# Normalise-and-project stages of a transformer kernel: the two halves of the tokens taken in another order

## The reference

```python
x = x + L0_xattn(_layernorm(x, axis=-1), ctx_768, ...)
x = x + L0_attn(_layernorm(x, axis=-1), ...)
x = x + L0_ffn(_layernorm(x, axis=-1), ...)
...
```

## Time and profile before

| | before |
|---|---|
| median of 3 runs | 2348.39 us (2341.73 to 2354.28) |
| the profiled execution | 2342.55 us |
| its span, first to last instruction | 2340.7 us |
| PE busy | 75% of the span |
| DVE busy | 46% |
| ACT busy | 32% |
| POOL busy | 22% |
| TensorE's granted clock, mean | 0.84 of full speed |

### The profile page before, as it was taken

One profiled execution on the slowest core, in us unless ns is written; L12 is line 12 of the kernel. 1 busy time (PEld: TensorE's weight loads), 2 busy tenths in 40 slices (PEclk: granted clock), 3 DMA queues, 4 the chain that ended last, 5 costly groups with the idle time before them and its releaser, 6 DMA issues. The chain is left out here.

```text
span 2340.7 us, 55956 instructions
## 1 busy us (share of the span) xinstructions
PE 1745.5 (75%) x22746; PEld 1508.6 (64%) x22746; DVE 1082.4 (46%) x2292; ACT 760.0 (32%) x1679; POOL 521.9 (22%) x683
## 2 busy tenths in 40 slices
PE   5997537689957886847884799673898676867684
PEld 4886436579946775637774688553787565756673
DVE  5565572411147775162114466537466445334313
ACT  3554332134424453302332455322142222323121
POOL 3442321022223331003442222100021222010142
PEclk9998755689979998758997899986889898776697
DMA  3110000179921110017995111001011211000385
GB/s 135 53 48 15 1 1 4 43 283 342 351 85 52 44 38 5 3 57 244 309 301 194 29 47 45 21 0 39 26 45 55 55 54 45 3 2 4 126 282 180
DMA packets 86641, 214.54 MB, mean 92 GB/s; under 512 B 20113, under 2 KB 38897, under 8 KB 78897
## 3 DMA queue, kind: packets, MB, share of 16 engines
q1 hardware_dynamic: 78288, 189.43, 24.8%
q0 software_dynamic: 8160, 22.29, 2.9%
HBM read 196.17 MB, written 15.34 MB: 90 GB/s over the span
## 5 line engine op out<-in xcount | busy, mean ns | idle before, releaser
L2184 ACT ACTIVATE g<-ps,b 128x128 f32<-128x128 f32 x340 | 125.0, 368 | 286.6 <-PE ps L2146 265.5
L2146 PEld LDWEIGHTS ps<-xt,w 128*128 128x128 f32 x1728 | 212.2, 197 | 8.3 <-issue 4.1
L2146 PE MATMUL ps<-xt,w 128*128 128x128 f32 x1728 | 213.3, 280 | 2.2 <-DVE xt L2325 2.1
L2156 PE MATMUL ps<-w,g 128*128 128x256 f32 x864 | 202.9, 382 | 0.0
L2156 PEld LDWEIGHTS ps<-w,g 128*128 128x128 f32 x864 | 158.4, 191 | 18.4
L449 PE MATMUL ps<-x,w 128*128 128x512 f32 x432 | 132.8, 476 | 38.9 <-DVE x L538 38.9
L2202 POOL DMA_INDIRECT x<-rows,token x85 | 83.3, 980 | 307.3 <-DVEq L2301 273.6
L2207 POOL DMA_INDIRECT results<-y,dest x85 | 83.7, 985 | 280.9 <-DVE y L2338 223.0
L2325 DVE COPY xt<-ps 128x256 f32<-128x256 f32 x85 | 36.1, 425 | 235.8 <-PE ps L2136 235.8
L449 PEld LDWEIGHTS ps<-x,w 128*128 128x128 f32 x432 | 100.9, 238 | 68.5 <-DVE x L538 44.6
L433 PE MATMUL ps<-consts_sb,z_sb 128*128 128x128 f32 x176 | 35.3, 370 | 115.0 <-DVE z_sb L524 115.0
(11 more groups left out here) (411 smaller groups left out, 4042.3 us busy)
## 6 DMA issues: line engine op xcount, KB each, us to landing
w<-in_L_ffn_w SPq DMA_DIRECT2D x124, 512.0 KB, 4.9
w<-in_L_ffn_w SPq DMA_DIRECT2D x46, 1024.0 KB, 7.4
c<-in_ctx SPq DMA_DIRECT2D x128, 258.0 KB, 2.7
b<-in_w_L_ffn SPq DMA_DIRECT2D x62, 128.0 KB, 6.5
back<-results SPq DMA_DIRECT2D x16, 256.0 KB, 5.0
raw<-in_L_ffn_w SPq DMA_DIRECT2D x16, 256.0 KB, 2.8
rows<-z_sb SPq DMA_DIRECT2D x3, 1024.0 KB, 4.4
back<-results SPq DMA_DIRECT2D x8, 384.0 KB, 6.5
```

The lines of the kernel that those rows point to most:

```text
L2146: mm = nc.tensor.matmul(hidden_bank(par, h), b.w1[:, par, c, h * P:(h + 1) * P], b.xt[:, par, c, :], start=c == 0, stop=c == DC - 1)
L2156: mm = nc.tensor.matmul(k.ps[:, YB + par, 0:D], b.g[:, par, h, :], b.w2[:, par, h, :], start=h == 0, stop=h == HC - 1)
L2184: nc.scalar.activation(b.g[:, par, h, :], hidden_bank(par, h), func, bias=b.b1[:, par, h:h + 1]).then_inc(s.g_ready, 1)
```

## The change

Only `prepare` is edited. In each of its 14 calls:

- ACT first waits for the `eps` constant, runs a one-column square root (`b.warm`) and then rounds the first weight matrix only. It takes the deviation of the first half, copies the first half's turned activations, takes the deviation of the second half, rounds the other weight matrices, evicts the first product if it owns it, copies the second half's turned activations and evicts the rest.
- DVE takes the statistics of the first half, normalises it, takes the statistics of the second half, computes the first half's low parts, normalises the second half, evicts the first product if it owns it, computes the second half's low parts and evicts the rest. Without products the order is: statistics, norm, statistics, norm, and the two copies at the end.
- PE turns the first half, makes the first unit of the first half, turns the second half, makes the other units of the first half and those of the second.
- POOL and SP are unchanged.

```diff
+            turn(0)
+            if units:
+                product(0, 0)
+            turn(1)
+            for n in range(1, len(units)):
+                product(0, n)
+            for n in range(len(units)):
+                product(1, n)
...
+            act.wait_ge(s.eps_set, 1)
+            nc.scalar.activation(b.warm[:], b.eps[:], ACT.Sqrt)
+            if w_at:
+                act.wait_ge(*w_at)
+            if ws:
+                round_weights(0)
+            deviation(0)
+            take_turned(0)
+            deviation(1)
+            for n in range(1, len(ws)):
+                round_weights(n)
+            if units:
+                take_product(0, 0)
+            take_turned(1)
+            for n in range(1, len(units)):
+                take_product(0, n)
+            for n in range(len(units)):
+                take_product(1, n)
...
+            nc.vector.memset(b.eps[:], LN_EPS).then_inc(s.eps_set, 1)
+            statistics(0)
+            norm(0)
+            statistics(1)
             if w_at:
                 dve.wait_ge(*w_at)
...
+            if jobs:
+                split(0)
+            norm(1)
+            if jobs:
+                take_product(0, 0)
+                split(1)
+                for n in range(1, len(units)):
+                    take_product(0, n)
+                for n in range(len(units)):
+                    take_product(1, n)
+            else:
+                take_turned(0)
+                take_turned(1)
```

More of the change, by code:

```diff
@@ L396, in prepare @@
     with stage(k, names) as (block, s), ExitStack() as ctx:
-        b = ctx.enter_context(buffers(k, stats=[P, NT, 6], mv=[P, NT, 2], std=[P, NT], rstd=[P, NT], eps=[P, 1]))
+        b = ctx.enter_context(buffers(k, stats=[P, NT, 6], mv=[P, NT, 2], std=[P, NT], rstd=[P, NT], eps=[P, 1], warm=[P, 1]))
         if jobs:
@@ L428, in _, with turn @@
         def _(pe):
-            for half in range(2):
+            def turn(half):
                 for t in range(HT):
@@ L435, in _, with product @@
                 mm.then_inc(s.turned, 1)
[L436 to L444, removed]
+            def product(half, n):
+                kind, wi, _, _, _, at = units[n]
+                if n == 0:
+                    pe.wait_ge(s.x_lo, DC * (half + 1))
+                if half == 0:
+                    pe.wait_ge(s.w_split, wi + 1)
+                turn_ = half * len(units) + n
+                if turn_ >= BANKS:
+                    pe.wait_ge(*taken((turn_ - BANKS) % len(units), (turn_ - BANKS) // len(units)))
+                bank = k.ps[:, 4 + turn_ % BANKS, :]
+                if kind == "channel":
+                    col = starts[wi] + at * P
@@ L445, in _ @@
                     for i, (p1, p2) in enumerate(TERMS):
                         for c in range(DC):
[L447 to L450, removed]
-                                                      start=i == 0 and c == 0, stop=i == 2 and c == DC - 1)
@@ L452, in _ @@
[L452 to L459, removed]
@@ L460, in _ @@
-                    mm.then_inc(s.product_done, 1)
+                            mm = nc.tensor.matmul(bank, r.w[:, p1, c, col:col + P],
+                                                  r.x[:, p2, c, half * 512:(half + 1) * 512],
+                                                  start=i == 0 and c == 0, stop=i == 2 and c == DC - 1)
+                else:
+                    for t in range(2):
+                        tok = (half * HT + 2 * at + t) * P
+                        for i, (p1, p2) in enumerate(TERMS):
+                            for c in range(DC):
+                                mm = nc.tensor.matmul(bank[:, t * D:(t + 1) * D], r.x[:, p1, c, tok:tok + P],
+                                                      r.w[:, p2, c, starts[wi]:starts[wi] + D],
+                                                      start=i == 0 and c == 0, stop=i == 2 and c == DC - 1)
@@ L462, in _ @@
+                mm.then_inc(s.product_done, 1)
+            turn(0)
[6 more added lines that the diff above has]
+                product(1, n)
         @block.scalar
         def _(act):
[L464 to L467, removed]
@@ L468, in _, with round_weights, deviation @@
-            act.wait_ge(s.eps_set, 1)
-            for half in range(2):
+            def round_weights(n):
+                nc.scalar.copy(r.w[:, HI, :, starts[n]:starts[n + 1]], ws[n]).then_inc(s.w_hi, 1)
+            def deviation(half):
                 tiles = slice(half * HT, (half + 1) * HT)
@@ L472, in _, with take_turned @@
                 nc.scalar.activation(b.std[:, tiles], b.mv[:, tiles, 1], ACT.Sqrt, bias=b.eps[:, 0:1]).then_inc(s.std_done, 1)
-            for half in range(2):
+            def take_turned(half):
                 tokens = slice(half * 512, (half + 1) * 512)
@@ L487, in _, with take_product @@
                             nc.scalar.activation(out, inp, ACT.Identity, bias=shift[:, c:c + 1], scale=gain[:, c:c + 1])
[L488 to L498, removed]
+            def take_product(half, n):
+                kind, _, _, bias, scale, m = units[n]
+                if owner[n] == "dve":
+                    return
+                act.wait_ge(s.product_done, half * len(units) + n + 1)
+                out, inp = view(n, half)
+                if kind == "token":
+                    nc.scalar.copy(out, inp).then_inc(s.taken_act, 1)
+                elif bias is None:
+                    nc.scalar.mul(out, inp, scale).then_inc(s.taken_act, 1)
+                else:
+                    nc.scalar.activation(out, inp, ACT.Identity, bias=bias[:, m:m + 1]).then_inc(s.taken_act, 1)
+            act.wait_ge(s.eps_set, 1)
[16 more added lines that the diff above has]
+                take_product(1, n)
         @block.gpsimd
@@ L510, in _, with statistics @@
         def _(dve):
-            nc.vector.memset(b.eps[:], LN_EPS).then_inc(s.eps_set, 1)
-            for half in range(2):
+            def statistics(half):
                 for t in range(half * HT, (half + 1) * HT):
@@ L517, in _, with norm @@
                     nc.vector.bn_aggr(b.mv[:, t, :], b.stats[:, t, :]).then_inc(s.aggr_done, 1)
-            for half in range(2):
+            def norm(half):
                 tiles = slice(half * HT, (half + 1) * HT)
@@ L525, in _, with split @@
                                             ALU.subtract, ALU.mult).then_inc(s.norm_done, 1)
+            def split(half):
+                tokens = slice(half * 512, (half + 1) * 512)
+                for c in range(DC):
+                    whole = k.ps[:, 2 * half + c, :]
+                    if gain is not None:
+                        whole = f.x[:, c, tokens]
+                        dve.wait_ge(s.x_gained, DC * half + c + 1)
+                        nc.vector.tensor_copy(r.x[:, HI, c, tokens], whole).then_inc(s.x_hi, 1)
+                    dve.wait_ge(s.x_hi, DC * half + c + 1)
+                    nc.vector.tensor_tensor(r.x[:, LO, c, tokens], whole, r.x[:, HI, c, tokens],
+                                            ALU.subtract).then_inc(s.x_lo, 1)
```

22 lines of the change are left out of this document (added).

## The result

| | before | after |
|---|---|---|
| median | 2347.65 us (6 runs, 2339.26 to 2357.32) | 2326.64 us (6 runs, 2320.35 to 2330.18) |
| ratio, with 95% interval | | 0.9907 (0.9884 to 0.9930) |
| the profiled execution's span | 2340.7 us | 2327.6 us |
| sum of the 14 calls of `prepare` in it | 316.3 us | 286.7 us |

Two further comparisons of the same pair gave 0.9899 (0.9842 to 0.9955) and 0.9900 (0.9880 to 0.9920). The medians differ by 21.0, 21.4 and 21.8 us; the three ratios, put on the medians of before, stand for 21.8, 23.7 and 23.5 us. The change gains some 22 us, or 0.9 to 1.0%.

A forecast was written before the change was run, and what follows sets the result against it. A chain through several engines, not one engine, was taken to bound `prepare`. Terms 5.5 + 18.2 - 3.3 + 9.6 - 3.8 = 26.2 us turn a median of 2348.4 into 2322.2 us; range 2309 to 2339.

The forecast's parts named there:

- The start: Nine calls with products: earlier table load and first-half norms bring the first product sooner, 5.5 us gained in sum.
- The second gap: PE's idle time before the second half's products, 19.1 us in nine calls, would be covered by first-half products: 18.2 us gained.
- the stall in L0_attn: With 5 weights, POOL's weight instructions delay the second norms; PE stands 1.5 us amid transposes, with clock loss -3.3 us.
- The clock: Second-half products of six calls ran partly at the lower clock; without the idle time before, 9.6 us gained.
- The calls without products: Five calls lose, as second statistics stand between the norms and the second deviation follows the first copy: -3.8 us.
- The sum within the calls: All terms in the 14 `prepare` calls together: 26.2 us gained, the calls falling from 316 to about 290.
- Outside the calls: Barriers enclose each call, so what a call loses or gains was taken to reach the end of the kernel.
- Rival 3: In nine calls transposes don't lift the clock, so low level lasts longer: 21 us lost, 2343 us; chance 0.06.
- Rival 1: The clock falls all the same in the second half, so the 9.6 us is not gained: 2331.8 us; chance 0.15.
- rival 2: Second-half turning stalls in every call with 3 or 5 weights, held by POOL: 15 us, 2337 us; chance 0.13.
- rival 4: Transposes with short waits keep PE's clock low through first halves of nine calls: 38 us lost, slower; chance 0.04.
- The alternation of POOL and norm: In `prepare`, a held norm passes between two POOL instructions, one norm per 1.3 us beside the weight instructions.

The follow-up runs named there:

- norms_only: Changed kernel, but PE makes all first-half products before turning the second half, as before, so only the new start is kept; ratio 1.0003 to the kernel before.
- interleave_only: Kernel before with only the second half's transposes moved behind the first product; old order of statistics, norms, weights and late table load; ratio 0.9861.
- clear_late: Changed kernel with POOL's clearing of `vt` held back until all eight norms are done; executed once, no ratio; 14 calls 277.3 us.
- no_warm: Changed kernel without the one-column square root and the `eps` wait ahead of it; executed once, no ratio; 14 calls 285.8 us.
- best_second: Second run of changed kernel with old order in calls without products, `vt` clearing after eighth norm, POOL's first weight instruction after fourth norm; ratio 0.9824 to before.

## Why the prediction was right or wrong

The forecast was -26.2 us; the comparisons gave -21.8, -23.7 and -23.5 by their ratios, and 21.0 to 21.8 by the medians. The direction, the range and the chain were right, the size 10 to 25% too large. By its own steps, with means of three profiles on each side:

- **The start**, 5.5 us: 85.1 to 79.8, so 5.3. Call by call: L1_attn 1.1 (0.8), L0_attn 3.1 (2.9), L1_xattn -1.3 (-1.2), L2_xattn -1.1 to -1.4 (-1.35), L3_xattn 0.6 (0.3), L0_xattn 0.0 (0.3), L3_attn 0.9 and L3_gqa 1.2 (1.0 each). L2_attn was missed: about 1.0 for 1.8. There POOL's second weight instruction held not only a norm but the second low part (L567), whose inputs both lie in SBUF: it took 1.64 us instead of 0.69.
- **The second gap** less the stall in L0_attn, 18.2 - 1.5 = 16.7 us: idle time from 19.1 to 2.3, so 16.8. The stall was 1.28 us in the first profile (0.45 + 0.83), 0.69 in the second. The 2-unit calls kept 0.1 to 0.6 us each.
- **The clock**, 9.6 less 1.75 = 7.9 us: 26.6 to 19.2, so 7.4. The mechanism is borne out: in all ten profiles of kernels with the turning, the second half's products of all nine calls stand at a granted clock of 1.00, while in before's three profiles six, six and four of the nine fell below it, and in norms_only, which keeps the gap, seven. What I had taken for a fixed six thus varies, and so do the calls that it strikes; its three profiles cost 28.9, 27.5 and 23.3 us. What decides whether a second half falls after the gap stays open.
- **The calls without products**, -3.8 us: -4.2.
- **The sum within the calls**, -26.2: 313.7 to 287.2, that is -26.6. The four measured terms make 25.3; the other 1.3 us is in none of them.
- **Outside the calls**, taken as 0. This is the step that failed. The rest was 2029.4 us before and 2036.9 after in the mean of three profiles, which takes back 7.6 us, while the whole times fall 3 to 6 us short of the sum within the calls. The sentence "what a call loses or gains reaches the end" left out that the same code outside the calls need not take the same time; convolve shows 1.1 us of that, with its clock, and the cause of the rest is open. That the sum within the calls came out within 0.4 us is in part luck: before's three profiles alone differ by 6.2 us there.

Rival 3 (transposes don't lift the clock) is out: in interleave_only the eight transposes stand within the low stretch, L1_attn's were done in 1.35 us against 1.91 at the low level, and the lower clock cost less in all, 16.8 and 18.7 us, than in before. Rival 1's loss of 9.6 didn't come, rival 2's stall only in L0_attn, and rival 4's low first halves not at all. The alternation of POOL and norm (one norm passes between two POOL instructions), on which the start rested, was confirmed by the first four norms in L2_xattn (6.35 us), of which one ended behind L536 and the next behind the clearing, and clear_late confirmed that the clearing holds them.

What I took for the cause of the late deviation was half wrong. In before, the table load came right behind the last cast or behind the statistics, whichever was later; I read it as tied to the deviation's wait, and no_warm shows that it need not be. So the square root was not needed for the start: no_warm's first products came at 76.0 us in sum, against 79.8 with it. L3_xattn, with one weight either way, points to the place of the `eps` wait and not to the number of weights rounded first, but no run tests the two apart.

## What to carry to other kernels

Where an engine waits in the middle of a stage for others to prepare its next input, put the request for that input one unit of work earlier in its own queue: here that one move was the gain, because the idle time and the clock's fall after it went together. Before a GpSimd instruction is placed, look at which normalisations it would hold on VectorE; a wait that puts it behind them can be worth more than starting either sooner. An order that helps where products follow can cost where none do, so each kind of call is to be costed by itself. And compare the whole times with the sum of the parts: here the parts promised 26.6 us and the whole gave 21 to 24.

## What the runs showed of the hardware that I had not expected

- An `ACT_TABLE_LOAD` (1.28 us) can run ahead of the data that its activation waits for: in no_warm it started 0.95 us before the statistics were complete (915.79 against 916.74). In before's L3_xattn, with the `eps` wait between the cast and the activation's own, it started only 0.08 us behind the statistics, 1.20 us after the cast.
- VectorE's subtraction with both inputs in SBUF was held by a GpSimd instruction like a norm (1.64 us instead of 0.69, the changed kernel's L2_attn), while two with one input in PSUM took 1.29 us together, unheld, beside L541 in best_second's L2_xattn.
- The lower level of TensorE's clock reaches over a barrier from one stage into the next. The same 32 matmuls of `convolve`, behind a call at a granted clock of 0.50, took 16.5 to 16.9 us or 17.6 to 18.05, at a mean granted clock of 0.89 to 0.91 or 0.83 to 0.85.
